# Recurrent scan and hyperbolic attention block on one core: head factors as one vector on VectorE and ScalarE, values on VectorE, key copies on ScalarE, attention groups only in chosen steps and twelve of them behind the scan

## The reference, cut to what matters

```python
def step(h, xt):
    m = concatenate([xt, h]) @ weight + bias
    c, g = tanh(m[:, 128:]), sigmoid(m[:, :128] + 1.0)
    h_new = g * h + (1.0 - g) * c
x = x + scan(step, cond, x)
xm = expmap0(layer_norm(logmap0(x)) * (1 + sc_msa) + sh_msa)
q, k, v = (_to_heads(plin(xm, w, b)) for w, b in (q, k, v))
attn = softmax(logmap0(q) @ logmap0(k).T / sqrt(8))
...
x = mobius_add(x, ...)
x = x + mobius_add(...)
```

## Time and profile before

| what | us |
|---|---|
| median of 3 runs (470.84 to 471.77) | 471.64 |
| the profiled execution, its own time | 471.58 |
| its span, first to last instruction | 469.8 |
| PE, DVE, ACT, POOL busy | 357.0, 314.5, 211.6, 136.4 |
| mean granted TensorE clock, share of full | 0.926 |

### The profile page before, as it was taken

One profiled execution on the slowest core, in us unless ns is written; L12 is line 12 of the kernel. 1 busy time (PEld: TensorE's weight loads), 2 busy tenths in 40 slices (PEclk: granted clock), 3 DMA queues, 4 the chain that ended last, 5 costly groups with the idle time before them and its releaser, 6 DMA issues.

```text
span 469.8 us, 14104 instructions
## 1 busy us (share of the span) xinstructions
PE 357.0 (76%) x5250; PEld 248.2 (53%) x5250; DVE 314.5 (67%) x1945; ACT 211.6 (45%) x965; POOL 136.4 (29%) x283
## 2 busy tenths in 40 slices
PE   1998999798767886857999999977669989737300
PEld 1655676576645665645666665654434545527200
DVE  6454444675877576777566687644852478999995
ACT  2223422224334225334435444545478899544350
POOL 6000000021282012183011147114430034455772
PEclk9999999999999999999999999999759998975655
DMA  7200930000000000000000000000000000000003
GB/s 179 59 1 4 200 72 3 2 28 22 1 2 3 1 3 1 1 3 1 2 3 1 3 3 2 1 3 2 2 1 3 1 1 4 2 0 1 1 0 90
DMA packets 9114, 8.42 MB, mean 18 GB/s; under 512 B 1275, under 2 KB 7693, under 8 KB 9046
## 3 DMA queue, kind: packets, MB, share of 16 engines
q1 hardware_dynamic: 8950, 7.26, 6.7%
q0 software_dynamic: 96, 0.26, 0.2%
HBM read 6.45 MB, written 1.08 MB: 16 GB/s over the span
## 4 chain that ended last, share of the span: by engine, by line
PE 55%; DVE 26%; ACT 11%; issue 5%; POOL 1%; DMA 1%; SPq 0%; DVEq 0%; ACTq 0%; POOLq 0%
PE zb L798 20%; PE tb L914 5%; DVE prod_hi L1462 4%; PE tb L745 4%; PE zb L776 4%; PE firsts L967 3%; ACT state L1202 3%; PE firsts L951 3%; DVE prod_lo L1468 2%; PE tb L893 2%; PE firsts L1077 2%; ACT state L1205 2%; ACT prd L1342 2%; PE firsts L798 2%; PE zb L782 1%
## 5 line engine op out<-in xcount | busy, mean ns | idle before, releaser
L798 PEld LDWEIGHTS zb<-prod_hi,whh 128*128 128x128 f16 x1920 | 73.2, 106 | 92.7 <-DVE prod_hi L1462 85.6
L1202 ACT ACTIVATE state<-zb 128x8 f32<-128x8 f32 x240 | 42.7, 178 | 166.3 <-PE zb L798 166.0
L798 PE MATMUL zb<-prod_hi,whh 128*128 128x8 f16 x1920 | 90.6, 171 | 34.4 <-DVE prod_hi L1462 33.3
L1462 DVE SCALAR_TENSOR_TENSOR prod_hi<-state 128x16 f16<-128x16 f32 x255 | 47.5, 186 | 94.1 <-ACT state L1205 91.5
L798 PE MATMUL zb<-prod_lo,whh 128*128 128x8 f16 x960 | 63.6, 172 | 1.5
L1468 DVE TENSOR_TENSOR prod_lo<-prod,prod_hi 128x16 f16<-128x16 f32 x255 | 48.9, 192 | 8.7
L798 PEld LDWEIGHTS zb<-prod_lo,whh 128*128 128x128 f16 x960 | 44.5, 107 | 4.7 <-DVE prod_lo L1468 1.8
L592 POOL TENSOR_TENSOR stat<-mv 128x4 f32<-128x4 f32 x4 | 0.8, 206 | 150.8 <-DVE mv L1557 150.8
L1342 ACT ACTIVATE prd<-zb 128x640 f32<-128x640 f32 x64 | 41.4, 719 | 5.7 <-PE zb L1057 5.3
L1464 DVE SCALAR_TENSOR_TENSOR prod<-state 128x16 f32<-128x16 f32 x256 | 43.3, 169 | 0.5 <-ACT state L1205 0.5
L1205 ACT ACTIVATE state<-zb 128x16 f32<-128x16 f32 x240 | 42.8, 178 | 0.0
(11 more groups left out here) (326 smaller groups left out, 720.0 us busy)
## 6 DMA issues: line engine op xcount, KB each, us to landing
mod<-ada_rows SPq DMA_DIRECT2D x4, 768.0 KB, 11.3
resid<-in_x_dram SPq DMA_DIRECT2D x6, 128.0 KB, 3.6
ffz<-shift_rows SPq DMA_DIRECT2D x4, 131.0 KB, 3.2
out_dram<-state SPq DMA_DIRECT2D x8, 64.0 KB, 2.1
out_dram<-early SPq DMA_DIRECT2D x8, 64.0 KB, 2.1
yy<-in_L_cond_w_ada_dram SPq DMA_DIRECT2D x1, 384.0 KB
early<-in_L_cond_weight_dram SPq DMA_DIRECT2D x2, 128.0 KB
resid<-in_x_dram POOLq DMA_DIRECT2D x2, 128.0 KB, 3.5
```

Of the source, the lines that this page charges most:

```text
L798: i = pe.matmul(z_bank(t, k)[:, NB * (t % CH):NB * (t % CH) + NB], whh[:, half, p, k, :], src[:, NB * p:NB * p + NB], start=False, stop=Fa ...
L1202: act.activation(r[:, 24:32], z_bank(t, 1)[:, k:k + NB], ACT.Tanh, scale=-1.0 / ZS)
L1462: dve.scalar_tensor_tensor(prod_hi[:, :], r[:, 16:32], 1.0, r[:, 0:16], ALU.add, ALU.mult).then_inc(hi_ready, 1)
```

## The change

Eight things change.

1. `hsum`, `hy`, `ht`, `hi32` become one vector of 204 numbers for a chunk. For chunks 0 to 2 DVE clamps and seeds (step offset 42), ACT squares `hy` three times (offsets 43, 45, 47), DVE does the two other instructions of each round, one a step, and `hfac` at 49. Chunk 3 does all of it on DVE.
2. For chunks 0 to 2 the values (two 64x128 products for each tile) go from POOL to DVE at offsets 62 to 65, the key copies from DVE to ACT at 58, 61, 63 and 65. Scale, high, low, stack and queries start six steps later.
3. The transposes of the next chunk wait for three of the four key copies, the second bank for all four.
4. `att_groups` starts at step 198 and leaves out the steps in `BUSY`; 20 groups lie before step 254, the other 12 go behind the scan, at due numbers `late`, `late_exps`, `late_values`, `late_saved`.
5. `x_part(2)` and `x_part(3)` start at `64(c-1) + 8` instead of `+ 4`.
6. The residual adds of pairs 0 to 2 go from POOL to DVE.
7. All due numbers behind the scan are new: the tables below give some of them.
8. Semaphores: `k_stack_last`, `v_scaled_last` for the last chunk, `root_r`, `root_t` in place of `factor_bits`, `roots`.

```diff
-    utrans=26, ... factor=(38, 43), scale=(44, 45, 50, 51), high=(45, 46, 53, 54), low=(46, 48, 54, 56),
-    stack=(48, 50, 56, 58), queries=(50, 52, 58, 60), keys=(52, 53, 59, 61), values=(50, 52), xna=21)
+    utrans=26, ... factor=42, scale=(50, 51, 56, 57), high=(51, 52, 57, 59), low=(52, 54, 58, 60),
+    stack=(54, 56, 60, 62), queries=(56, 60, 62, 64), keys=(58, 61, 63, 65), values=(62, 63, 64, 65),
+    xna=21, hfac=49)
...
+BUSY = frozenset((193, 194, 195, 196, 218, 219, 220, 221, 222, 223, 224, 225, 226, 227, 246, 247, 248, 249, 252, 253, 254, 255))
 def att_groups():
-    out = []
+    out, t = [], 198
     for b in range(NB):
         for i in range(NI):
-            t = tok_base(1) + 54 + 2 * (NI * b + i)
-            out.append((b, i, t if t < tok_base(2) + 28 else t + 8))
+            while t in BUSY or t + 1 in BUSY:
+                t += 1
+            out.append((b, i, t))
+            t += 2
...
-                    for q in range(2):
-                        yield from at_ticks(now, base + T["factor"][q])
-                        if (c, q) != (NC - 1, 1):
-                            pool.wait_ge(factor_bits, 2 * c + q + 1)
-                            head_factors(pool, q, settled, False).then_inc(roots, 1)
...
-                            pool.wait_ge(block_out, NC * j + NC)
-                            pool.tensor_tensor(T_R[j], T_R[j], view(resid[:, j, 0:1], [NJ * D, NC], [1, D]),
-                                               ALU.add).then_inc(res_ready, 1)
...
-                    yield from at_ticks(now, CH * (c - 1) + 4)
+                    yield from at_ticks(now, CH * (c - 1) + 8)
...
+                for g in range(NSCAN, len(GROUPS)):
+                    yield from at_ticks(now, STEPS + DIAG["late"][g - NSCAN])
+                    scores(g)
+                    yield from at_ticks(now, STEPS + DIAG["late_values"][g - NSCAN])
+                    values(g - 1)
...
+                    def keys(j):
+                        act.wait_ge(stack_ps, NJ * c + j + 1)
+                        act.activation(key_part(c, j), key_stack(j), ACT.Copy).then_inc(k_stack, 1)
+                    if c < NC - 1:
+                        for k in range(3):
+                            yield from at_ticks(now, base + T["factor"] + 1 + 2 * k)
+                            act.wait_ge(root_r, 3 * c + k + 1)
+                            act.activation(ht[:, :], hy[:, :], ACT.Square).then_inc(root_t, 1)
...
+            def head_factors(now, c, base, T):
+                x, r, t = hsum[:, :], hy[:, :], ht[:, :]
+                settle()
+                done_(dve.tensor_scalar(x, x, 1.2e-38, None, ALU.max))
+                i = dve.tensor_scalar(r.bitcast(I32), hi32[:, :], -1.0, float(0x5F3759DF), ALU.mult, ALU.add)
+                for k in range(3):
+                    if in_scan:
+                        i.then_inc(root_r, 1)
+                        yield
+                        dve.wait_ge(root_t, 3 * c + k + 1)
...
+                        done_(dve.scalar_tensor_tensor(t, t, -0.5, x, ALU.mult, ALU.mult))
+                    if in_scan:
+                        mark = done[0]
+                        yield
+                        settle(mark)
+                    i = dve.scalar_tensor_tensor(r, t, 1.5, r, ALU.add, ALU.mult)
...
+                        yield from at_ticks(now, base + T["add"][p])
+                        dve.wait_ge(block_out, NC * j + NC)
+                        dve.tensor_tensor(T_R[j], T_R[j], view(resid[:, j, 0:1], [NJ * D, NC], [1, D]),
+                                          ALU.add).then_inc(res_ready, 1)
```

More of the change, by code:

```diff
@@ L76 @@
     uevac=28, usq=(26, 27), clip=29, qkv=(29, 30, 31, 32, 33, 34, 35, 36), yevac=(31, 33, 35,
-    37), qsq=(32, 34, 36, 38), qreduce=(34, 36, 38, 40), factor=(38, 43), scale=(44, 45, 50,
-    51), high=(45, 46, 53, 54), low=(46, 48, 54, 56), stack=(48, 50, 56, 58), queries=(50, 52,
-    58, 60), keys=(52, 53, 59, 61), values=(50, 52), xna=21)
+    37), qsq=(32, 34, 36, 38), qreduce=(34, 36, 38, 40), factor=42, scale=(50, 51, 56, 57),
+    high=(51, 52, 57, 59), low=(52, 54, 58, 60), stack=(54, 56, 60, 62), queries=(56, 60, 62,
@@ L80 @@
+    64), keys=(58, 61, 63, 65), values=(62, 63, 64, 65), xna=21, hfac=49)
 TOK_LAST = dict(
-    transpose=20, resid=39, moments=47, norm=60, artanh=81, rho=127, xn=143, modulate=152,
-    utrans=163, uevac=182, usq=(161, 170), clip=176, qkv=(192, 199, 205, 212, 215, 218, 226,
-    231), yevac=(207, 217, 228, 243), qsq=(214, 223, 234, 249), qreduce=(222, 233, 248, 255),
-    factor=(244, 246), scale=(313, 319, 341, 348), high=(320, 326, 360, 366), low=(327, 335,
-    367, 374), stack=(336, 344, 375, 456), queries=(346, 355, 391, 477), keys=(353, 361, 398,
@@ L112 @@
[L112 to L122 removed]
+    transpose=23, resid=44, moments=52, norm=65, artanh=87, rho=134, xn=150, modulate=162,
@@ new lines @@
+    utrans=175, uevac=209, usq=(172, 182), clip=189, qkv=(217, 229, 241, 247, 257, 261, 271,
+    275), yevac=(234, 252, 266, 280), qsq=(241, 263, 277, 291), qreduce=(262, 272, 285, 296),
+    factor=(310, 328), scale=(356, 360, 389, 393), high=(361, 372, 416, 427), low=(368, 382,
+    423, 435), stack=(379, 399, 431, 444), queries=(398, 411, 438, 474), keys=(404, 417, 446,
+    480), values=(357, 376), xna=153, transpose_=36, utrans_=198, stack_=(392, 405, 434, 447),
+    resid_=48, moments_=56, artanh_=(93, 95, 97, 100, 102, 105, 107, 109, 111, 113, 115, 116,
@@ L136 @@
[L136 to L140 removed]
[3 rows of a table removed]
[L144 to L151 removed]
+    ot=(1068, 1076), o=(1081, 1090), oT=(1099,), oevac=(1110,), wo=(1117,), m=(1133,),
@@ L344, in ugrnn_block_kernel @@
         GROUPS = att_groups()
+        NSCAN = sum(1 for g in GROUPS if g[2] < 254)
         load_scan, load_x0 = sem("load_scan"), sem("load_x0")
@@ L971, in attention @@
                 pe.wait_ge(pool_init, 1)
-                for g in range(len(GROUPS)):
+                for g in range(NSCAN):
                     yield from at_ticks(now, GROUPS[g][2])
@@ L1317, in attention @@
                 for g, (b, i, tick) in enumerate(GROUPS):
-                    yield from at_ticks(now, tick + 1)
+                    if g < NSCAN:
+                        yield from at_ticks(now, tick + 1)
+                    else:
+                        yield from at_ticks(now, STEPS + DIAG["late_exps"][g - NSCAN])
                     act.wait_ge(scores_ready, g + 1)
```

284 lines of the change are left out of this document (149 added, 135 removed), and 6 rows, old and new, of the table scores.

## The result

The changed kernel takes 469.09 us (median of 7 runs, 466.39 to 469.31) against 471.64 for the kernel before (7 runs beside it): ratio 0.9932, interval 0.9917 to 0.9947. So it is faster by 0.7%, 3.2 us by the ratio and 2.6 by the two medians, where I had forecast 9.5; 469.09 lies above my range.

A forecast was written before the change was run, and what follows sets the result against it. It took the PE, ACT, DVE, PE chain of each step to pace the scan, then DVE in the tails and the output queue. -15.3 + 3.4 + 2.4 = -9.5 from 471.58 gave 462.1 us, range 457.0 to 468.5.

The forecast's parts named there:

- Scan: The whole recurrence: 15.3 us shorter, 280.0 instead of 295.3, from factors and values, x part and attention groups.
- Factors and values: Scan from offset 37 of chunks 0 to 2: POOL's work leaves, 2.57 us gained a chunk, 7.7 in all.
- the x part's 0.6: Scan step 132: x matmuls start four steps later, apart from the last transposes, gaining 0.6 us.
- the groups that met the stack transposes: Scan steps 184 to 187 and 248 to 251: attention groups there lose 1.66 us each time; the new list avoids them.
- Rival (1): Scan: new pieces stand in the recurrence's way, 0.22 us a step, 4.6 in all, giving 466.7 us; chance 0.16.
- Before the diagonals: Between scan and diagonals: twelve late groups, 16.0 us unhidden, partly fill PE's idle time; diagonals start 8.2 us later.
- The lower bound of 2.8: Smallest delay of the diagonals: sixteen and twelve groups of 1.33 us, 2.0 of transposes, all else hidden.
- Diagonals and tails: Behind the first diagonal: part of the delay is regained, so DVE's last instruction comes 3.4 us later after the scan.
- The adds' share: Tails: DVE gains 3.1 us without POOL's residual adds and pays 1.9 for doing three itself.
- rival (3): Clock stays full through the late groups; growth behind the scan is 3.5 us less, giving 458.6 us; chance 0.13.
- Output queue: End of the kernel: SP's transfers end 7.1 us after DVE instead of 4.7, 2.4 us longer.
- Rival (2): Behind the scan: the twelve groups are not hidden, diagonals and tails shift by 16.0 us, giving 473.5; chance 0.10.

The follow-up runs named there:

- c1: Changed kernel plus 24 spare 128x102 POOL products a chunk from offset 37 of chunks 0 to 2, nothing waiting for them: 475.34 us (one run).
- d6: Changed kernel with 28 groups in the scan, four late, q, k, v matmuls together, both saves of the third pair due inside the head factors: 466.94 us, 0.9906.
- d5: Changed kernel with 28 groups in the scan, four late, sixteen q, k, v matmuls together, one save moved into the head factors: 466.55 us, 0.9912.
- b1: Changed kernel with all 32 groups in scan steps 190 to 252, none late, and the kernel before's due numbers behind the scan: 465.55 us, 0.989.
- b4_adds_on_pool: Changed kernel with the residual adds of pairs 0 to 2 back on POOL: 465.12 us, 0.9878.
- a3_save_early: Changed kernel with one DVE save of the third queries put in front of chunk 3's head factors instead of inside them: 467.54 us, 0.9922.

## Why the prediction was wrong

**Scan: right.** Forecast -15.3, measured -16.3. Factors and values: 2.57 a chunk forecast, 2.68 measured in chunks 0 and 1 (19.74 to 17.06), and c1 shows the hold by itself: 24 products alone bring 2.03 of them back. The stretch of 64 steps that holds steps 184 to 187 gained 4.96, which is 2.68, the x part's 0.6 and the 1.66 of the groups that met the stack transposes. Rival (1) didn't occur: all pieces of 204 numbers (0.27 and 0.37 us) fit. Step 228 stayed at 1.79, step 234 at 1.35 (the save), 242 to 244 at about 1.24, as priced.

**Before the diagonals: the step that failed.** The prediction said "Hidden is what fills the wait at the end of this stage: PE is busy 24.1 of 36.2 us" and read off the due numbers that "the diagonals start 8.2 us later". They start 12.3 later. Three readings were wrong. I counted PE's idle time as room, but the part at its end is a wait for the chain of modulated rows, q, k, v, head factors, queries and keys, and late groups and the third queries behind them push this chain as well: with 4 groups the first diagonal is 5.9 later (d6), with 12 the keys are ready 9.3 later than before. And "the q, k, v matmuls can now lie in the 0.47 gaps" holds for the order but not for the price: between third queries a pair takes 1.01 us, in a block 4.54 / 7 = 0.65 a pair (d5), and the sixteen, at the head of the chain, are spread over 10.8 us where b1 has 5.1. Third, of the 12.3 us, 3 are third queries that still stand ahead of the first diagonal when its keys are there. The due numbers gave an order; I used them as times for a stretch in which they had never been run. 4.1 of the 5.8 us by which the growth behind the scan exceeds my sum are here. The lower bound of 2.8 was also added up wrong: 28 groups of 1.33 and 2.0 of transposes are 39.2, 3.0 over 36.2.

**Diagonals and tails.** From the first diagonal to DVE's last instruction I forecast 4.8 us back (8.2 to 3.4) and 3.6 came (12.3 to 8.6): 1.2 short. The adds' share came: taking them off POOL was to give DVE 1.2 us net, and b4_adds_on_pool shows 1.5. The full clock did come in the profiled execution, 1.00 against 0.91 in the diagonal window, but the diagonals took only 1.0 us less, because ACT is busy 52.7 of 58.7 us. The kernel before, first diagonal to the same point:

```profile
345.20:404.90 59.70, 54.31 (x865) 30.61 (x866) 33.69 (x205) 53.26 (x134) 10.52 (x21) 0.91 0.01 2
```

That is also what became of rival (3). The clock was full in the diagonals and that was worth 1.0; 7.4 us of half clock there cost 1.3 in c1_pool_products, not the 3.5 I gave as a bound. Its premise, the full clock through the late groups, wasn't met, and its ground, "the full clock from 309 to 327", was no reading of the clock: the kernel before has no entry until 331.9, and the 0.63 us of L1015 in the earlier trace rows is the duration at half clock. Behind the first entry, at a recorded 1.00, the same sixteen take:

```profile
333.60 0.42 PE L1015 MATMUL firsts<-prd,V 128*18 128x64 f32 x16 [0.47 <-ACT prd L1332]
```

So 1.33 us a group was a price at half clock, and fitted (1.36) because the late groups ran at it too. The rule of the Trainium skill, "TensorE: Matmul & The Clock Gate", section "What's actually happening", that I weighed in the prediction can't be relied on by itself: in a3_save_early PE was busy 9.85 of 10.2 us at a mean clock of 0.52.

**Output queue.** Forecast 2.4, measured 2.9 (7.65 instead of 4.71 from DVE's end). Mechanism right, 0.5 short.

**Rival (2)** comes nearest: groups not hidden, chain and third queries queue behind them. It gave 16.0 for the shift; 12.3 came. Its decision point was a growth of 15.3; it was 11.6, so the kernel stayed on the faster side.

**The rest.** By its spans the change saves 4.7 us, by the ratio 3.2. The seven spans lie from 464.6 to 467.5, and the profiled one is among the shortest. Their mean clocks of 0.905 to 0.942 say little, since the time before the first entry counts as full in them (the 0.926 of the kernel before too). What the traces do show is that the scan repeats to 0.2 us, and that half clock in the diagonals makes up to 2.6 us (table under a3_save_early). What sets its place from one execution to the next stays open.

**Better versions.** `b4_adds_on_pool` (465.12) and `b1_all_in_scan` (465.55) beat the kernel before by 1.1 to 1.2% and the changed one by about half of a per cent, each with one part of the change undone. Parts 1, 2, 3 and 5 together carry the gain (none was run alone); the late groups give back what they bring, and the adds' place costs. Both undone at once wasn't tried; b1_all_in_scan, with its adds on DVE at the old due numbers, ends 5.9 us behind DVE's last instruction, so little is left to gain there.

## What to carry to other kernels

Idle time in front of a stage is room only for work that doesn't stand ahead of the chain which ends that idle time; ask what the wait is for, and whether the moved work delays it on the way. Work moved out of one chain into "free" time ahead of another can cost its full length if both run on one in-order engine (against b1, four groups, 5.4 us of work, put the diagonals 5.9 us later, and twelve, 16.3 us, 12.6): price it so, and take hiding as the rival. Look at what then stands between the pieces of the chain. Take from a table of due numbers the order, not the times. And before a clock is read from a view, see where its entries begin, and check it by the duration of one matmul form.

## What the runs showed of the hardware

- A POOL product holds DVE's short instructions with two SBUF inputs from 0.17 to 0.34 us; a POOL memset of the same tile doesn't.
- Two 128x192 fp32 matmuls cost 1.01 us as a pair between other work and 0.65 us a pair in a block of fourteen (d5, both before that trace's first clock entry at 324.6, where the matmuls have the durations of half clock).
- Four 32x128 score matmuls took 0.58 us at a recorded clock of 0.50 and 0.38 at 1.00; sixteen 128x64 value matmuls 0.63 and 0.42. By these durations the whole scan ran at half clock (0.58 at 246.71), where the view prints 1.00 for want of an entry.
- Half clock for 0, 2.0, 7.4 and 10.2 us of the diagonals made them 58.6, 58.9, 59.9 and 61.2 us long.
- PE was busy 9.85 of 10.20 us in a window whose clock was 0.52, and 9.79 in the next, at 1.00.
